# Attention and mixture-of-experts kernel on one core: projections on other slots, three buffers of probabilities, value products in bursts of two key tiles

## The chip, the cores and the metric

The kernel runs on one core of a Trainium2 chip. The metric is the device time of one execution in microseconds (us). A core has TensorE (PE; PEld is its loading of weights), VectorE (DVE), ScalarE (ACT) and GpSimd (POOL); SyncE (SP) only issues transfers here. Each runs its own list of instructions in order, and they wait for each other by semaphores.

## The reference

For 8 sequences of 512 tokens of width 256:

```
x = x + tanh(g_xattn) * attention(q=layernorm(x), k=ctx, v=ctx)     # "cross": 16 heads of 16, softmax over 512 keys
z = layernorm(x)
h = z + (causal attention with rotary embedding of rmsnorm(z)*g1, projections wq, wk, wv) @ wo   # "own"
y = h + moe(rmsnorm(h) * g2)                                         # softmax router, best 2 of 8 experts, hidden 704
x = x + tanh(g_ffn) * y
```

All is float32. The experts compute (silu(t @ wg) * (t @ wu)) @ wd.

## The kernel before

**Attention.** There are 16 units of attention, 8 cross and 8 own, in the order of `UNITS` (cross of sequence b+2, then own of b). A unit has 4 groups of 4 heads. The program goes in steps -1 to 7 of 8 **stages** each, s0 to s7. A stage holds 16 **slots** (4 key tiles `kt` by 4 heads `hd`). Slot numbers in the tables run through a step: slot 16 s + 4 kt + hd. In each stage three groups are in work:

- the maxima of one group (`max_unit`): PE multiplies queries with keys into one of 3 banks `max_ps`, and DVE reduces each to a row maximum (`neg`, L1274). Stages s0 to s3 do this for a cross unit (512 keys), s4 to s7 for an own unit (128 to 512 keys, plus a small product with a mask).
- the main work of a group whose maxima are two stages old (`key_unit`, `exp_unit`, `value_unit`): PE makes the transposed scores in one of 2 banks `key_ps`; the maxima are three extra rows of `q_stack`. ACT takes the exponential into `probs` (L1155), and PE multiplies the values with the probabilities into `pv_ps` (L984), four heads side by side in 32 columns of the array each. In s0 and s1 that is an own unit, in s2 to s5 a cross unit, in s6 and s7 an own unit.
- between both, the maxima are split in three by POOL (`split_neg`, L1604 to L1607), turned by PE (L997, after `kt` 1), copied by ACT to `neg_rows` (L1230, before `kt` 2) and sent to `q_stack` by a DMA. `key_unit` of the next stage waits for it. A finished group is copied to `out_t` (L1225), turned by PE (L1009) and divided by DVE (`post_norm`).

The four value products of a key tile stand after slot `hd` 1 of the next key tile:

```
if hd == VALUES_AT:
    for each in range(HG):
        if kt == 0 and tail: value_unit(step, tail, QT - 1, each)
        if kt and mn:        value_unit(step, mn, kt - 1, each)
```

**Everything else** is put on slots by hand. `X_TURNS`, `HN1_TURNS`, `Q_HALVES`, `K_HALVES`, `V_HALVES`, `WO_HALVES`, `LOGITS`, `RANKS` and the like say at which slot of which step PE begins a transpose or a half of a projection. They all go through one bank, `aux`, one after the other: `aux_turn` makes PE wait until the one before is taken out, which ACT does two slots after a transpose (`evacuate`, L1161), and DVE three slots after a half of q or k (`rotation`: a product with the cosines, L1311, and a shuffle, L1313, which frees the bank). POOL multiplies, adds and splits what DVE left in `turned` and `with_cos` (`rotate`, L1614, L1615), at the stages of `ROTATE_STAGES`. POOL also splits inputs and the experts' weights (`split_piece`), normalises rows (`hn2_rows`, `x1_rows`), adds up (`base_rows`) and scatters rows; `HN2_STAGE`, `BASE_STAGE`, `SCATTER_STAGES` and `PIECES_IN_STEP` give the stages. SP loads the stacks of the next units (`load_stack`, six DMAs each) and waits for `key_ps` products before each.

**Experts.** After the last step the rows are gathered by expert in 71 tiles of 128, each with an up product, a gate and a down product, PE after PE.

Of the kernel before, what the change touches and what calls it, by code (L numbers as in the profile page):

```python
# [20 lines left out]
ALU = mybir.AluOpType  # L21
# [8 lines left out]
E, F = 8, 704  # L30
# [28 lines left out]
VALUES_AT = 1  # L59

# [76 lines left out]
def stage(i, s):  # L137
# [6 lines left out]
X_STATS = {b: at(b - 4, 68) if b > 2 else at(-1, 36) for b in range(2, B)}  # L144
X_TURNS = {1: at(-1, 2, 6), 2: at(-1, 50, 54), 3: at(0, 44, 48), **{b: at(b - 3, 4, 8) for b in range(4, B)}}
C_TURNS = {1: at(-1, 26, 30), 2: at(-1, 66, 70), 3: at(0, 52, 56), **{b: at(b - 3, 26, 30) for b in range(4, B)}}
X1_SUMS = {b: at(b - 2, 118, 128) for b in BATCHES} | {0: at(-1, 112, 114), 1: at(0, 46, 48), LAST: at(LAST - 2, 112, 114)}
X1_ENDS = {b: at(b - 1, 4) for b in BATCHES} | {0: at(-1, 116), 1: at(0, 50), LAST: at(LAST - 2, 116)}
HN1_ROWS = {b: at(b - 1, 20) for b in BATCHES} | {0: at(0, 0), 1: at(0, 60), LAST: at(LAST - 1, 0)}
HN1_TURNS = {b: at(b - 1, 72, 76) for b in REGULAR_OWN} | {0: at(0, 4, 8), LAST - 1: at(LAST - 2, 44, 48), LAST: at(LAST - 1, 4, 8)}  # L150
Q_HALVES = {b: at(b - 1, 80, 85) for b in REGULAR_OWN} | {0: at(0, 12, 17), LAST - 1: at(LAST - 2, 52, 57), LAST: at(LAST - 1, 12, 17)}
K_HALVES = {b: at(b - 1, 105, 117) for b in REGULAR_OWN} | {0: at(0, 22, 27), LAST - 1: at(LAST - 2, 82, 87), LAST: at(LAST - 1, 22, 27)}
V_HALVES = {b: at(b, 33, 38) for b in BATCHES} | {LAST - 1: at(LAST - 2, 118, 123), LAST: at(LAST - 1, 33, 38)}
ATT_TURNS = {b: at(b + 1, 52, 56) for b in BATCHES} | {LAST - 3: at(LAST - 2, 62, 66), LAST - 1: at(LAST - 1, 114, 118), LAST: at(LAST, 48, 52)}
WO_HALVES = {b: at(b + 1, 60, 66) for b in BATCHES} | {LAST - 3: at(LAST - 2, 70, 75), LAST - 1: at(LAST - 1, 122, 128), LAST: at(LAST, 56, 61)}
# [3 lines left out]
LOGITS = {b: at(b + 1, 98) for b in BATCHES} | {LAST - 3: at(LAST - 2, 102), LAST - 1: at(LAST, 27), LAST: at(LAST, 87)}
CHOICES = {b: at(b + 1, 100, 102, 104) for b in BATCHES} | {LAST - 3: at(LAST - 2, 104, 106, 108), LAST - 1: at(LAST, 29, 31, 33),  # L160
                                                          LAST: at(LAST, 89, 91, 93)}
RANKS = {b: at(b + 1, 110) for b in BATCHES} | {LAST - 2: at(LAST - 1, 107), LAST - 1: at(LAST, 36), LAST: at(LAST, 96)}
PLACES = {b: at(b + 1, 113, 115, 122) for b in BATCHES} | {LAST - 2: at(LAST - 1, 109, 110, 112), LAST - 1: at(LAST, 39, 40, 41),
                                                         LAST: at(LAST, 98, 99, 100)}

XQ_STAGE = {b: stage(b - 4, 4) if b > 2 else stage(-1, 2) for b in range(2, B)}
# [7 lines left out]
HN2_STAGE = {b: stage(b + 1, 4) for b in BATCHES} | {LAST - 3: stage(LAST - 2, 5), LAST - 1: stage(LAST, 0), LAST: stage(LAST, 4)}  # L174
BASE_STAGE = {b: stage(b + 1, 5) for b in BATCHES} | {LAST - 1: stage(LAST, 1), LAST: stage(LAST + 1, 0)}
SCATTER_STAGES = {b: (stage(b + 2, 5), stage(b + 2, 6)) for b in BATCHES} | \
    {LAST - 4: (stage(LAST - 2, 2), stage(LAST - 2, 3)), LAST - 3: (stage(LAST - 1, 2), stage(LAST - 1, 4)),
     LAST - 2: (stage(LAST - 1, 7), stage(LAST, 0)), LAST - 1: (stage(LAST, 3),) * 2, LAST: (stage(LAST, 7),) * 2}
PIECES_IN_STEP = {-1: (0, 0, 1, 1, 1, 1, 1, 1), 0: (2, 0, 0, 0, 1, 2, 2, 2), LAST - 2: (0, 0, 2, 2, 0, 0, 2, 1),
                  LAST - 1: (2, 0, 0, 2, 1, 2, 2, 1), LAST: (0,) * 8}  # L180


def pieces_in(st):

    count = lambda n: PIECES_IN_STEP.get(n // 8, (0, 0, 0, 2, 3, 2, 1, 0))[n % 8]
    done = sum(count(n) for n in range(stage(-1, 0), st))
    return range(done, done + count(st))
# [86 lines left out]
def flamingo_block(nc, x, ctx, g_xattn, g_ffn, wq, wk, wv, wo, w_router, wg, wu, wd, g1, g2, out):  # L274
# [25 lines left out]
    with outer:  # L300
# [23 lines left out]
        with ExitStack() as st:  # L324
# [20 lines left out]
            probs = s1("probs", 2, HG, S)  # L345
# [18 lines left out]
            turned = {"q": s1("turned_q", DC, S), "k": s1("turned_k", DC, S)}  # L364
            with_cos = {"q": s1("with_cos_q", DC, S), "k": s1("with_cos_k", DC, S)}
# [377 lines left out]
            def _(sp):  # L743
# [87 lines left out]
                def body(step):  # L831
# [12 lines left out]
                    if i + 3 < B:  # L844
                        load_ctx(i + 3)
# [910 lines left out]
```

## Time and profile before

| | |
|---|---|
| times of three runs | 1591.45, 1581.02, 1590.68 us, median 1590.68 us |
| profiled execution | 1575.98 us, of which the span of instructions is 1573.6 us |
| PE, PEld, DVE, ACT, POOL busy in the span | 1433.8, 881.3, 975.2, 777.3, 879.7 us |
| stretch of attention, 40 to 1023 us | PE busy 918.77, DVE 673.77, ACT 593.38, POOL 714.83 us |
| between attention and experts, 1023 to 1078 us | PE busy 17.88 us, its clock 0.53 of full speed |
| experts, 1078 to 1573.6 us | PE busy 482.50 us |
| mean TensorE clock | 0.976 |

A busy share is the time in which an engine had an instruction in work. A matmul's span in the trace includes its way through the array; how much time it takes from its engine is the distance from its start to the start of the next. The start of each copy to `out_t` (once in a stage, at `kt` 1) is used as a mark, so a stretch between two marks is one stage long; the stretch called s3 runs from `kt` 1 of s2 to the end of `kt` 0 of s3. In step 2 the marks stand at 373.57, 388.15, 400.64, 415.43, 430.65, 447.30, 463.29, 481.07 and 494.83 us.

### The profile page before, as it was taken

The numbers are of one execution on the slowest core, as the hardware profiler recorded it, in microseconds if no ns is written. First come the engines' busy times: TensorE is split into PE (matmuls) and PEld (weight loads), VectorE is DVE, ScalarE is ACT, GpSimd is POOL, SyncE is SP. The second block draws the span as 40 slices with busy tenths as digits, with TensorE's granted clock in tenths as the row PEclk, the third lists the DMA queues.
The fourth block names the chain that finished last, engine by engine and source line by source line (L and its number), as shares of the span: only waits on it lengthen the run. The fifth ranks groups of instructions, "written<-read, shape, count | busy, mean of one in ns | idle before, by whom it ended". The sixth has DMA issues, their size and how long they took to land.

```text
span 1573.6 us, 31721 instructions
## 1 busy us (share of the span) xinstructions
PE 1433.8 (91%) x9439; PEld 881.3 (56%) x9439; DVE 975.2 (62%) x2329; ACT 777.3 (49%) x1782; POOL 879.7 (56%) x1147
## 2 busy tenths in 40 slices
PE   3999999999999999999899998845999999999997
PEld 1232334344444444444444454434999999999996
DVE  5888767757767766766866656324555555555553
ACT  1576665665665664665566555611333333333332
POOL 7485776974977977877879676533222222222222
PEclk9999999999999999999999999957999999999999
DMA  7665356565565574664553646146252454355220
GB/s 198 187 173 174 106 177 180 169 209 143 153 204 166 167 218 148 180 181 163 175 187 103 210 136 192 68 166 207 38 150 53 136 151 143 47 152 149 40 42 11
DMA packets 116517, 230.19 MB, mean 146 GB/s; under 512 B 20101, under 2 KB 82949, under 8 KB 114310
## 3 DMA queue, kind: packets, MB, share of 16 engines
q1 hardware_dynamic: 76114, 147.65, 31.2%
q0 software_dynamic: 26032, 69.82, 15.8%
q10 hardware_dynamic: 14212, 10.71, 2.7%
q8 instruction: 86, 1.41, 0.4%
q14 instruction: 73, 0.60, 0.1%
HBM read 135.10 MB, written 93.14 MB: 145 GB/s over the span
## 4 chain that ended last, share of the span: by engine, by line
PE 68%; POOL 9%; DVE 8%; issue 5%; ACT 4%; DMA 4%; SPq 1%; ACTq 0%; POOLq 0%; DVEq 0%
PE pv_ps L984 9%; PE pv_ps L713 9%; PE max_ps L689 9%; PE key_ps L689 9%; PE max_ps L946 8%; PE key_ps L963 8%; DVE neg L1274 4%; PE aux L1032 3%; PE aux L1023 3%; ACT probs L1155 2%; PE turn_ps L702 2%; PE aux L1016 2%; POOL rows_in L1681 2%; DMA q_stack<-neg_rows 2%; POOL w_parts L1578 1%
## 5 line engine op out<-in xcount | busy, mean ns | idle before, releaser
L1274 DVE TENSOR_REDUCE neg<-max_ps 128x1 f32<-128x512 f32 (+3 forms) x864 | 543.5, 666 | 278.9 <-PE max_ps L949 177.3
L1155 ACT ACTIVATE probs<-key_ps 128x512 f32<-128x512 f32 (+3 forms) x1024 | 497.1, 519 | 366.8 <-PE key_ps L963 176.1
L946 PE MATMUL max_ps<-k_stack,q_stack 96*128 96x512 bf16 (+3 forms) x1024 | 356.1, 352 | 30.8 <-DVE neg L1274 16.2
L963 PE MATMUL key_ps<-q_stack,k_stack 99*128 99x512 bf16 (+3 forms) x1024 | 350.3, 343 | 24.4 <-ACT probs L1155 16.0
L556 POOL DMA_INDIRECT out<-part,whose x71 | 110.1, 1551 | 377.4 <-DVE part L589 304.9
L946 PEld LDWEIGHTS max_ps<-k_stack,q_stack 96*128 96x128 bf16 x1024 | 100.8, 99 | 219.3 <-DVE neg L1274 123.0
L963 PEld LDWEIGHTS key_ps<-q_stack,k_stack 99*128 99x128 bf16 x1024 | 100.2, 98 | 131.0 <-ACT probs L1155 70.0
L713 PE MATMUL pv_ps<-weights,hidden_t 128*128 x1207 | 161.9, 288 | 1.4 <-DVE hidden_t L609 1.4
L689 PE MATMUL max_ps<-weights,rows_t 128*128 x642 | 153.7, 385 | 2.8 <-DVE rows_t L580 2.8
L689 PE MATMUL key_ps<-weights,rows_t 128*128 x636 | 150.3, 381 | 1.0 <-DVE rows_t L580 1.0
L713 PEld LDWEIGHTS pv_ps<-weights,hidden_t 128*128 128x128 f32 x1207 | 149.0, 191 | 1.7 <-issue 1.7
L984 PE MATMUL pv_ps<-probs,v_cross 128*32 128x512 f32 (+3 forms) x1024 | 132.3, 588 | 3.4 <-ACT out_t L1225 2.3
L689 PEld LDWEIGHTS max_ps<-weights,rows_t 128*128 128x128 f32 x642 | 117.8, 191 | 22.9 <-issue 3.2
L689 PEld LDWEIGHTS key_ps<-weights,rows_t 128*128 128x128 f32 x636 | 115.1, 189 | 20.2 <-issue 1.2
L949 PE MATMUL max_ps<-squares_b 128*128 128x128 bf16 x512 | 113.2, 221 | 0.0
L966 PE MATMUL key_ps<-squares_b 128*128 128x128 bf16 x512 | 112.6, 220 | 0.0
L653 ACT ACTIVATE hidden_t<-turn_ps 128x512 fp32r<-128x512 f32 x71 | 42.4, 597 | 135.5 <-PE turn_ps L702 133.3
L984 PE MATMUL pv_ps<-probs,v_own 128*32 128x512 f32 (+3 forms) x1024 | 102.6, 470 | 3.1 <-ACT out_t L1225 2.0
L1604 POOL TENSOR_SCALAR neg_parts<-neg 128x16 bf16<-128x16 f32 x64 | 16.0, 250 | 154.9 <-DVE neg L1274 145.8
L1578 POOL TENSOR_TENSOR w_parts<-w_in,w_parts 128x704 fp32r<-128x704 f32 (+2 forms) x64 | 85.9, 1343 | 5.4
L628 ACT ACTIVATE rows_t<-max_ps,g_sb 128x128 fp32r<-128x128 f32 x142 | 44.4, 364 | 85.7 <-PE max_ps L666 65.6
L609 DVE TENSOR_TENSOR hidden_t<-turn_ps,hidden_t 128x512 fp32r<-128x512 f32 x71 | 49.1, 692 | 45.6 <-ACT hidden_t L653 45.6
(213 smaller groups left out, 2102.1 us busy)
## 6 DMA issues: line engine op xcount, KB each, us to landing
w_split<-w_parts POOLq DMA_DIRECT2D x32, 704.0 KB, 5.6
weights<-w_split SPq DMA_DIRECT2D x8, 2816.0 KB
weights<-w_split SPq DMA_DIRECT2D x8, 1280.0 KB
rows<-rows_in ACTq DMA_DIRECT2D x71, 129.0 KB, 2.1
w_split<-w_parts POOLq DMA_DIRECT2D x16, 512.0 KB, 3.6
kept_sb<-kept SPq DMA_DIRECT2D x16, 512.0 KB, 6.1
parts_cross_k<-parts_k SPq DMA_DIRECT2D x48, 128.0 KB
parts_cross_q<-parts_q SPq DMA_DIRECT2D x48, 128.0 KB
```

The lines of the kernel that those rows point to most:

```text
L556: g_.indirect_dma_start(out=out_rows, out_offset=bass.IndirectOffsetOnAxis(ap=whose[j % OWNERS][:, 0:1], axis=0), in_=part[j % OWNERS][:, ...
L609: v.tensor_tensor(lo[:, 0:4, :].rearrange("p k t -> p (k t)"), hid_ps[0][:, :], hi[:, 0:4, :].rearrange("p k t -> p (k t)"), ALU.subtract) ...
L689: r = mm(ps, rows_t[:, a, c, :], weights[:, bass.ds(off + (w_ * WALL + c * 2 * F + n0), n1 - n0)], start=(c == 0 and (a, w_) == PASSES[0]) ...
L713: r = mm(y_ps[:, 0:D], hidden_t[:, a, k, :], weights[:, bass.ds(off + (w_ * WALL + 2 * WG + k * D), D)], start=(k == 0 and (a, w_) == PASS ...
L946: r = mm(ps[:, 0:keys], q_stack[g][0:KROWS, hd, qt * P:(qt + 1) * P], k_stack[g][0:KROWS, hd, 0:keys], start=True, stop=not own)
L949: r = mm(ps[:, qt * P:keys], ident_b, mask_qk, start=False, stop=True)
L963: r = mm(ps[:, q0:S], k_stack[g][0:KROWS + NEGROWS, hd, kt * P:(kt + 1) * P], q_stack[g][0:KROWS + NEGROWS, hd, q0:S], start=True, stop=no ...
L966: r = mm(ps[:, q0:q0 + P], ident_b, mask_kq, start=False, stop=True)
L984: mm(pv_ps[32 * hd:32 * hd + 32, q0:S], v_of[value_tile(which, b)][:, kt, g * HG + hd, :], probs[:, kt % 2, hd, q0:S], start=(kt == 0), st ...
L1155: act.activation(probs[:, kt % 2, hd, q0:S], key_ps[j % 2][:, q0:S], ACT.Exp).then_inc(m["exp_done"], 1)
L1274: v.tensor_reduce(neg[:, g % 2, hd - place_:hd + 1, qt], scores, op=ALU.max, axis=AX.X, negate=True).then_inc(m["max_red"], many)
L1578: chain.link(g_.tensor_tensor(low, whole, high, ALU.subtract))
```

## The change

- `probs` has three places (`PROBS = 3`) in place of two, used in turn by all key tiles. The value products of two key tiles stand behind each other: those of tiles 0 and 1 after slot `hd` 1 of `kt` 2, those of 2 and 3 after slot `hd` 1 of `kt` 0 of the next stage.
- The slots of the side work are others. In a middle step the attention output's transposes and `wo` go from s3 and s4 to s5 and s6, the halves of q from s5 to s7, the halves of k from s6 and s7 to s0 and s1 of the next step, the second half of v from s2 to s3, `hn2`, router and ranks one step later from s5 to s7 to s4 to s6. POOL's `hn2_rows` and `base_rows` go to s7, and the weight pieces per stage are other numbers of the same total.
- To make room, `turned` and `with_cos` exist once, and not for q and k each; `rotation` waits for POOL to have read the half two before.
- The evacuations of `hn1` and `hn2` (four per sequence) go from ACT to DVE (`take_out`).
- The DMA of `neg_rows` is issued by SP and not by ACT.
- SP's `send_base` of the last steps stands elsewhere.

```diff
+PROBS = 3
-HN1_TURNS = {b: at(b - 1, 72, 76) for b in REGULAR_OWN} | ...
-Q_HALVES = {b: at(b - 1, 80, 85) for b in REGULAR_OWN} | ...
-K_HALVES = {b: at(b - 1, 105, 117) for b in REGULAR_OWN} | ...
+HN1_TURNS = {b: at(b - 1, 92, 95) for b in REGULAR_OWN} | ...
+Q_HALVES = {b: at(b - 1, 112, 120) for b in REGULAR_OWN} | ...
+K_HALVES = {b: at(b, 10, 24) for b in REGULAR_OWN} | ...
...
-            probs = s1("probs", 2, HG, S)
+            probs = s1("probs", PROBS, HG, S)
-            turned = {"q": s1("turned_q", DC, S), "k": s1("turned_k", DC, S)}
-            with_cos = {"q": s1("with_cos_q", DC, S), "k": s1("with_cos_k", DC, S)}
+            turned, with_cos = s1("turned", DC, S), s1("with_cos", DC, S)
...
+                def send_neg(step, s):
+                    unit = step.neg_of(s)
+                    if unit:
+                        n = unit[2] * G + unit[3]
+                        sp.wait_ge(m["neg_ev"], n + 1)
+                        sp.dma_start(q_stack[unit[3]][KROWS:KROWS + NEGROWS, :, :], neg_rows[:, :]).then_inc(m["neg_dma"], 16)
...
-                       probs[:, kt % 2, hd, q0:S], start=(kt == 0), stop=(kt == QT - 1), skip_group_check=True)\
+                       probs[:, (n * QT + kt) % PROBS, hd, q0:S], start=(kt == 0), stop=(kt == QT - 1), skip_group_check=True)\
...
-                                if hd == VALUES_AT:
-                                    for each in range(HG):
-                                        if kt == 0 and tail:
-                                            value_unit(step, tail, QT - 1, each)
-                                        if kt and mn:
-                                            value_unit(step, mn, kt - 1, each)
+                                if hd == VALUES_AT and kt % 2 == 0:
+                                    unit = mn if kt else tail
+                                    for k in (0, 1) if kt else (2, 3):
+                                        for each in range(HG) if unit else ():
+                                            value_unit(step, unit, k, each)
...
-                    step.wait(act, m["pv_mm"], n * 16 + (HG * (kt - 2) + hd + 1))
+                    step.wait(act, m["pv_mm"], n * 16 + (HG * (kt - PROBS) + hd + 1))
...
-                                step.wait(act, m["neg_ev"], n + 1)
-                                act.dma_start(q_stack[ng[3]][KROWS:KROWS + NEGROWS, :, :], neg_rows[:, :]).then_inc(m["neg_dma"], 16)
...
-                    over(dve, m["rope_used"], 4 * (b - 1) + k + 1)
+                    over(dve, m["rope_used"], 4 * b + k - 1)
...
+                def take_out(name, b, c, dst, scale):
+                    aux_full(dve, name, b, c)
+                    v.tensor_scalar(dst[:, c, :], aux[:, :], scale[:, c:c + 1], None, ALU.mult).then_inc(m["aux_free"], 1)
```

On PE, in a cross stage with cross maxima, the program before has a burst of four value products after every four pairs of `max_ps` and `key_ps` products:

```order
L984 MATMUL pv_ps<-probs,v_cross_57 32x512 x4
L946 MATMUL max_ps2<-k_stack2_55,q_stack2_51 128x512
L963 MATMUL key_ps0<-q_stack0_49,k_stack0_53 128x512
L946 MATMUL max_ps0<-k_stack2_55,q_stack2_51 128x512
L963 MATMUL key_ps1<-q_stack0_49,k_stack0_53 128x512
L1009 MATMUL turn_ps<-ident,out_t 128x128 x4
L946 MATMUL max_ps1<-k_stack2_55,q_stack2_51 128x512
L963 MATMUL key_ps0<-q_stack0_49,k_stack0_53 128x512
L946 MATMUL max_ps2<-k_stack2_55,q_stack2_51 128x512
L963 MATMUL key_ps1<-q_stack0_49,k_stack0_53 128x512
L984 MATMUL pv_ps<-probs,v_cross_57 32x512 x4
```

The changed program has eight there (two key tiles), and no burst for the next eight pairs; here half of them are shown, with the second half of v between:

```order
L1018 MATMUL pv_ps<-probs,v_cross_57 32x512 x8
L1066 MATMUL aux<-sb_wv,hn1_t 128x256 x2
L980 MATMUL max_ps1<-k_stack3_56,q_stack3_52 128x512
L997 MATMUL key_ps0<-q_stack1_50,k_stack1_54 128x512
L1066 MATMUL aux<-sb_wv,hn1_t 128x256 x2
L980 MATMUL max_ps2<-k_stack3_56,q_stack3_52 128x512
L997 MATMUL key_ps1<-q_stack1_50,k_stack1_54 128x512
L980 MATMUL max_ps0<-k_stack3_56,q_stack3_52 128x512
L997 MATMUL key_ps0<-q_stack1_50,k_stack1_54 128x512
L980 MATMUL max_ps1<-k_stack3_56,q_stack3_52 128x512
L997 MATMUL key_ps1<-q_stack1_50,k_stack1_54 128x512
L980 MATMUL max_ps2<-k_stack3_56,q_stack3_52 128x512
```

So half of the switches between scores and value products are gone, and the stretch of scores between two bursts is twice as long.

On PE in s1 of a middle step (own keys, cross maxima), the changed program has the second half of k (`sb_wk`), the burst, one pair, and then the transpose of `ctx_in` into the same bank `aux`:

```order
L1057 MATMUL aux<-hn1_t,sb_wk 128x512
L980 MATMUL max_ps0<-k_stack1_54,q_stack1_50 128x512
L997 MATMUL key_ps1<-q_stack3_52,k_stack3_56 128x256
L1000 MATMUL key_ps1<-squares_b 128x128
L1018 MATMUL pv_ps<-probs,v_own 32x512 x4
L1018 MATMUL pv_ps<-probs,v_own 32x384 x4
L980 MATMUL max_ps1<-k_stack1_54,q_stack1_50 128x512
L997 MATMUL key_ps0<-q_stack3_52,k_stack3_56 128x256
L1000 MATMUL key_ps0<-squares_b 128x128
L1050 MATMUL aux<-ident,ctx_in_59 128x128 x4
L980 MATMUL max_ps2<-k_stack1_54,q_stack1_50 128x512
L997 MATMUL key_ps1<-q_stack3_52,k_stack3_56 128x256
```

Before, the halves of k stand in s6 and s7 with no user of `aux` for twelve slots behind the second; here the next user comes at slot 27, the very slot at which DVE takes the half of k out.

On ACT, at `kt` 2 of each stage, the program before has the copy of the turned maxima and the issue of their DMA in a row:

```order
L1155 ACTIVATE probs<-key_ps1 128x512
L1230 ACTIVATE neg_rows<-turn_ps 48x128
L1232 DMA q_stack3_52<-neg_rows 3x16x128
L1155 ACTIVATE probs<-key_ps0 128x512
L1155 ACTIVATE probs<-key_ps1 128x512
```

The changed program has the DMA in SP's list, here between the six DMAs of a stack load and the next ones:

```order
L784 DMA k_stack2_55<-parts_cross_k 48x1x2048
L784 DMA k_stack2_55<-parts_cross_k 32x1x2048
L784 DMA k_stack2_55<-parts_cross_k 16x2048
L830 DMA q_stack0_49<-neg_rows 3x16x128
L789 DMA parts_own_q<-parts_q_61 8x16x512 x6
L784 DMA q_stack3_52<-parts_cross_q 48x1x2048
L784 DMA q_stack3_52<-parts_cross_q 32x1x2048
L784 DMA q_stack3_52<-parts_cross_q 16x2048
```

The issue is off ACT and stands in a queue that waits for other things too.

## Rows read from the trace of the kernel before

**Rows 1.** View by stretches, step 2, s0 to s7: length, each engine's busy us (instructions), clock, DMA.

```profile
373.57:388.15 14.58, 13.21 (x103) 6.20 (x101) 12.64 (x30) 7.25 (x19) 4.24 (x8) 1.00 0.44 121
388.15:400.64 12.49, 11.99 (x93) 5.63 (x93) 11.73 (x25) 8.29 (x22) 11.11 (x22) 1.00 0.60 168
400.64:415.43 14.79, 13.79 (x98) 6.91 (x96) 10.84 (x19) 9.43 (x25) 13.53 (x17) 1.00 0.74 242
415.43:430.65 15.22, 14.58 (x82) 5.81 (x81) 10.81 (x19) 10.31 (x21) 13.79 (x16) 1.00 0.32 87
430.65:447.30 16.65, 16.42 (x98) 7.73 (x96) 9.71 (x18) 10.35 (x21) 10.99 (x13) 1.00 0.77 219
447.30:463.29 15.99, 15.02 (x97) 6.56 (x97) 10.92 (x26) 11.94 (x29) 12.51 (x17) 1.00 0.63 211
463.29:481.07 17.78, 16.98 (x120) 8.56 (x119) 8.48 (x17) 10.39 (x22) 16.14 (x26) 1.00 0.64 207
481.07:494.83 13.76, 12.89 (x122) 6.72 (x120) 10.76 (x41) 7.18 (x20) 8.91 (x15) 1.00 0.40 125
sum 121.26, PE 114.88 PEld 54.12 DVE 85.91 ACT 75.13 POOL 91.21; mean PE 14.36 PEld 6.76 DVE 10.74 ACT 9.39 POOL 11.40
```

**Rows 2.** Timeline of PE in stretch s3 of step 2: start us, us, instruction, count.

```profile
424.60 0.38 PE L963 MATMUL key_ps<-q_stack,k_stack 99*128 99x512 bf16 x1
424.91 1.06 PE L984 MATMUL pv_ps<-probs,v_cross 128*32 128x512 f32 x8
425.91 0.39 PE L946 MATMUL max_ps<-k_stack,q_stack 96*128 96x512 bf16 x1
```

**Rows 3.** Timeline of PE in step 7, bursts of an own group.

```profile
1002.18 1.07 PE L984 MATMUL pv_ps<-probs,v_own 128*32 128x512 f32 x8 [0.18 <-ACT out_t L1225]
...
1009.93 0.43 PE L984 MATMUL pv_ps<-probs,v_own 128*32 128x128 f32 x8
```

**Rows 4.** Timeline of PE's weight loads around one burst.

```profile
510.86 0.16 PEld L984 LDWEIGHTS pv_ps<-probs,v_own 128*32 128x32 f32 x8 [0.21 <-ACT probs L1155]
```

**Rows 5.** Timeline of PE, side work and the next instruction.

```profile
458.30 1.02 PE L1023 MATMUL aux<-hn_t,sb_wq 128*128 128x512 f32 x2
459.16 0.22 PE L946 MATMUL max_ps<-k_stack,q_stack 96*128 96x128 bf16 x1
...
474.00 0.66 PE L1016 MATMUL aux<-ident,hn 128*128 128x128 f32 x4
474.49 0.38 PE L946 MATMUL max_ps<-k_stack,q_stack 96*128 96x512 bf16 x1
```

**Rows 6.** View by groups, shapes apart, whole span: busy us, mean ns, idle before.

```profile
L1274 DVE TENSOR_REDUCE neg<-max_ps 128x1 f32<-128x512 f32 x640 | 411.4, 684 | 121.6 <-PE max_ps L946 98.3 <-PE max_ps L949 21.3
L1155 ACT ACTIVATE probs<-key_ps 128x512 f32<-128x512 f32 x640 | 356.3, 599 | 224.5 <-PE key_ps L963 176.1 <-PE key_ps L966 46.1 <-ACT neg_rows L1230 0.9
...
L1614 POOL TENSOR_TENSOR turned_q<-turned_q,rope_sb 128x512 f32<-128x512 f32 x16 | 20.9, 1307 | 0.2
...
L1313 DVE STREAM_SHUFFLE turned_k<-aux 128x512 f32<-128x512 f32 x16 | 11.8, 738 | 0.0
...
L1311 DVE TENSOR_TENSOR with_cos_k<-aux,rope_sb 128x512 f32<-128x512 f32 x16 | 10.9, 681 | 0.0
```

**Rows 7.** Waits from 374 to 495 us: who for whom, total us, times, longest.

```profile
PEld key_ps L963 <- ACT probs L1155: 6.6, 17, 0.9
```

**Rows 8.** View of line 1232, the issue of the maxima's DMA: ns min/median/max.

```profile
L1232 ACTq DMA_DIRECT2D q_stack<-neg_rows x64: 728/729/900, 45.1 to 1005.1; - x64
```

**Rows 9.** Timeline of PE in stretch s6 of step 3.

```profile
591.08 0.24 PE L997 MATMUL turn_ps<-squares_b,neg_parts 128*48 128x128 bf16 x1 [2.30 <-POOL neg_parts L1607]
```

**Rows 10.** View by stretches: s6 of step 3, and 2 us in it.

```profile
584.64:605.81 21.17, 18.58 (x120) 9.23 (x119) 8.69 (x17) 10.49 (x22) 18.77 (x29) 0.92 0.60 181
594.00:596.00 2.00, 2.00 (x10) 1.33 (x10) 0.56 (x1) 0.24 (x1) 1.99 (x3) 0.50 0.30 61
```

**Rows 11.** Waits of SP's queue from 374 to 495 us.

```profile
SPq L776 <- PE key_ps L963: 34.5, 5, 12.2
```

More of the change, by code:

```diff
@@ L142 @@
 REGULAR_OWN = range(1, LAST - 1)
-X_STATS = {b: at(b - 4, 68) if b > 2 else at(-1, 36) for b in range(2, B)}
+X_STATS = {b: at(b - 4, 84) if b > 3 else at(-1, 68 if b == 3 else 36) for b in range(2, B)}
 X_TURNS = {1: at(-1, 2, 6), 2: at(-1, 50, 54), 3: at(0, 44, 48), **{b: at(b - 3, 4, 8) for b in range(4, B)}}
-C_TURNS = {1: at(-1, 26, 30), 2: at(-1, 66, 70), 3: at(0, 52, 56), **{b: at(b - 3, 26, 30) for b in range(4, B)}}
-X1_SUMS = {b: at(b - 2, 118, 128) for b in BATCHES} | {0: at(-1, 112, 114), 1: at(0, 46, 48), LAST: at(LAST - 2, 112, 114)}
@@ L159 @@
[L159 to L164, printed above, removed]
@@ L166 @@
-XQ_STAGE = {b: stage(b - 4, 4) if b > 2 else stage(-1, 2) for b in range(2, B)}
+HN1_TURNS = {b: at(b - 1, 92, 95) for b in REGULAR_OWN} | {0: at(0, 4, 8), LAST - 1: at(LAST - 2, 46, 50), LAST: at(LAST - 1, 4, 8)}
+Q_HALVES = {b: at(b - 1, 112, 120) for b in REGULAR_OWN} | {0: at(0, 12, 17), LAST - 1: at(LAST - 2, 54, 59), LAST: at(LAST - 1, 12, 17)}
+K_HALVES = {b: at(b, 10, 24) for b in REGULAR_OWN} | {0: at(0, 26, 34), LAST - 1: at(LAST - 2, 78, 83), LAST: at(LAST - 1, 26, 34)}
+V_HALVES = {b: at(b, 34, 50) for b in BATCHES} | {0: at(0, 41, 50), LAST - 2: at(LAST - 2, 33, 41), LAST - 1: at(LAST - 2, 118, 123),
+                                                  LAST: at(LAST - 1, 44, 49)}
@@ L167 @@
+XQ_STAGE = {b: stage(b - 4, 5) if b > 3 else stage(-1, 4 if b == 3 else 2) for b in range(2, B)}
 X_STAGE = {1: stage(-1, 0), 2: stage(-1, 4), **{b: stage(b - 3, 2 + (b == 3)) for b in range(3, B)}}
@@ L836, in body @@
                     if i == LAST:
+                        send_neg(step, 0)
                         send_base(LAST - 1)
@@ L865, in body @@
                     load_stack(step.half(1), 0)
+                    send_neg(step, 3)
                     if i + 4 < B:
@@ L874, in body @@
                     load_stack(step.half(1), 1)
+                    send_neg(step, 4)
                     if i + 3 < B:
@@ L877, in body @@
                     load_stack(step.half(1), 2)
+                    send_neg(step, 5)
                     if i == LAST - 2:
@@ L881, in body @@
                     load_stack(step.half(1), 3)
+                    send_neg(step, 6)
                     if i == LAST - 2:
@@ L886, in body @@
                         load_stack(step.half(2), 0)
+                    send_neg(step, 7)
                     if 0 < i < LAST - 1:
```

108 lines of the change are left out of this document (65 added, 43 removed).

## The prediction

> **What bounds the kernel now.** I read the page first (busy shares, then the clock row), then the view by stretches over one middle step, then timelines and waits within it. Attention runs to 1023 us and the experts from 1078 us; the change touches only the first part. In a middle step of 121.26 us PE is busy for 114.88 us, DVE for 85.91, ACT for 75.13 and POOL for 91.21 [rows 1]. So PE sets the step, but not in all stretches. The lengths go from 12.49 to 17.78 us, and the long ones (s4 16.65, s6 17.78) are those with most side work on PE: 16.42 and 16.98 us busy. In s0 and s1 the maxima are those of a cross unit and DVE has 12.64 and 11.73 us of work in 14.58 and 12.49: there DVE sets the pace and PE waits for banks, much of it in pieces too short to be idle in this view. In s6 POOL has 16.14 of 17.78. A saving on PE therefore counts in six stretches of eight, and hardly in s0 and s1.
>
> **Bursts of two key tiles.** What a switch costs: the last scores product before a burst starts at 424.60 and needs 0.22 us for its 512 columns (the spacing of such products here), so it is through at 424.82, and the next scores product starts at 425.91 [rows 2]: 1.09 us. The own bursts of 512 and of 128 columns last 1.07 and 0.43 us [rows 3], so 384 columns are worth 0.64 and 512 columns 0.85. The rest of 1.09 is 0.24, paid at each switch. Two tiles in a row pay it once. There are 64 groups with 4 bursts now and 2 then, so 128 switches go: 128 x 0.24 = 31 us of PE time. Of that three quarters lie in stretches that PE sets: **-23 us** (bounds -31, and 0 if the second tile can't follow without a gap).
>
> For the second tile to follow at once its weights must be loaded under the first one's products. In the trace all eight loads of a burst lie within 0.16 us at its start, the products take 1.06 [rows 2, 4]; so loads that use the same 128 rows and the same 32 columns do go under running products. The Trainium skill (TensorE: Matmul & The Clock Gate, Part 3, The mechanism) says that loading overlaps with running matmuls only when the row group differs; here all four heads use all rows. By that rule the gap between the two tiles would stay. By it the term would be 0; the trace speaks against the rule.
>
> **Longer stretches of scores.** Between bursts stand eight pairs and not four. An exponential of 512 columns takes 356.3/640 = 0.56 us of ACT's time [rows 6], a pair of PE only 2 x 0.22 = 0.44, and there are just two banks `key_ps`. So far a burst of 1.1 us let ACT catch up after four pairs. Now a burst of 1.9 us leaves ACT idle for 0.8 of it (two banks hold 1.1 us of work), and over eight pairs PE would run 8 x 0.12 = 1.0 us ahead and must wait. In the 8 half stages of a step with cross keys that is at most 8 us a step if nothing else stood between; but the turns of maxima and outputs and 1.3 us of side work on average stand in each half stage, and they give ACT that time. I take 1 us a step, **+8 us** for eight steps (bounds 0 and +40, the latter if side work covers only a third).
>
> **ACT's relief.** Each of the 64 issues of the maxima's DMA holds ACT for 0.73 us [rows 8] while exponentials wait, and four evacuations per sequence leave too. PE's loads waited 6.6 us for exponentials in that step [rows 7]. I take a third of it, 2 us a step: **-16 us** (bounds 0 and -53, all of it). The four evacuations cost DVE 0.68 each (a pass of the same size from a bank, [rows 6]), in s4 to s6, where DVE has 9.71, 10.92 and 8.48 us of work in 16 to 18 [rows 1]: nothing; in a stage that DVE sets they would cost 2.7 a step.
>
> **Levelling of the stretches.** `wo` and its transposes leave s4 (4 x 0.86 + 2 x 0.49 = 4.4 us by [rows 5]) for s5 to s7, the halves of k come to s1 and s2. Work that PE does in another stretch which PE sets too saves nothing. What saves is that the arithmetic of `PLACES` and half of `X1_SUMS` leave stretch s0, which DVE sets: s0 is 2.1 us longer than s1 with the same main work [rows 1], of which 0.7 is more side work on PE. I take the other 1.4 over five steps: **-7 us** (bounds 0 and -12). That s1 gets 1.7 us more of PE work and two passes of DVE (0.68 + 0.74) is on the other side and in the next term.
>
> **The bank `aux`.** Side work now follows itself more closely. At slot 27 PE wants `aux` for `ctx_in`, and at slot 27 DVE takes out the second half of k: DVE must first do the maximum of slot 26 (411.4/640 = 0.64), then 0.68 and 0.74 [rows 6], after a PE that reaches the place some 0.2 us after that maximum's scores. PE stops for about 1.9 us, where before it had twelve slots of distance. Slots 10, 86 to 98 have distances of 0 or 1 slot behind ACT or DVE, where two were the rule; I put 0.3 us on each of five. Together 3.4 us a step, five steps: **+17 us** (bounds 0, if PE would have waited for DVE there anyway, and +30).
>
> **POOL.** In step 3, `split_neg` came late, PE stood still for 2.30 us [rows 9], and the clock fell to half for some us (0.50, 1.2 GHz, from 594 to 596 us); that stretch took 21.17 us against 17.78 for the same one in step 2 [rows 1, 10]. `hn2_rows` and `base_rows` leave the full stages 4 and 5 for 7, where POOL has only 8.91 us of work. I count this case and half of one more: **-6 us** (bounds 0 and -12). SP takes over 64 issues; its queue waits 34.5 us of the step for keys to be read [rows 11], and the maxima have half a stage, 7 us, to land: nothing (bounds 0 and +20, if a store ahead in its queue is late by more than that).
>
> **Sum.** -23 + 8 - 16 - 7 + 17 - 6 = -27 us, against the profiled execution's 1575.98 us: 1549 us. The three runs have a median of 1590.68 us, 14.7 above the profiled one. I read the difference as more cases like step 3's (3.4 us each), of which POOL's relief removes about half: 1590.7 - 27 - 7.5 = **1556 us**.
>
> **Rivals.**
> *More than that* (0.15): the waits on `aux` lie where DVE sets the pace anyway, and ACT's relief gives 4 us a step: 1556 - 17 - 16 = 1523. For it speaks that s1 is DVE's; against it that slot 27 lies at the border of s2, which PE sets.
> *The clock falls at slot 27* (0.12): a wait of 1.9 us is close to the 2.30 after which it fell. Half clock for some 3 us costs 1.7 each time; in five steps, with waits of 1 us more behind it, +13: 1569.
> *The gaps stay* (0.15): the second tile's loads do not go under the first one's products, or the longer stretches cost what the bursts give. 23 us of gain are lost: 1579.
> *Slower: one buffer of rotation* (0.13). DVE's `rotation` of the first half of k at slot 13 must wait until POOL has read the first half of q in stage 0, of the second half at slot 27 until POOL has read that of q in stage 1. POOL needs two products of 1.3 us [rows 6] and two passes no longer than these, 5.2 us at most. It has 13/16 of a stage, 10.6 us, in the first case and 11/16, 9 us, in the second. With `hn2_rows`, `base_rows` and a weight piece now in s7 and two rotations in s1 (11.11 us of 12.49, [rows 1]), a POOL that is 4 us late or more makes DVE wait, and behind it the maxima and PE. If it is 6 us late, each case costs 2 us and half clock 1.7: 7.4 a step, six steps and their echo in the next maxima's split together +50: 1606. It decides from a lateness of 4 us on. Against it: POOL has 91.21 of 121.26 us of work, and the same total after.
> *The forecast* (0.45): 1556.
>
> **Range and chances.** Below 1520 I see only the bounds of ACT's term; above 1592 most of the slower rival. Leaving out both, the range is 1520 to 1592. About 1% (1575 to 1607) is what a measurement of this kernel can tell from no change. Faster by over 1%: the forecast's 0.45 less a tenth of it, 0.15, and nine tenths of the clock's 0.12: 0.66. Slower by over 1%: 0.08 of the slower rival and 0.02 from the gaps: 0.10. Within 1%: 0.24.
>
> **What would show it.** In the changed profile: 128 bursts with 16 products, of 1.9 us for cross groups (the gap's term wrong if 2.1 or more); a middle step of about 117 us with stretches from 13 to 16; PE idle of about 1.9 us before the transpose of `ctx_in` at slot 27; no half clock at `split_neg`; waits of PE for exponentials around 5 us a step. The prediction is wrong if DVE waits for POOL's `rope_used`, if `key_ps` products wait for the maxima's DMA, or if the waits for exponentials grow beyond 10 us a step.

## The result and the profile after

The changed kernel takes 1673.59 us (median of 4 runs, 1669.86 to 1674.14) against 1589.92 us before; the ratio is 1.0541, 95% interval 1.0511 to 1.0570: slower. Forecast were 1556 us, and even the slower rival's 1606 lay far below what came. In the profiles nearly all of it is lost in attention, which ends at 1119 us where it ended at 1023. The profiled execution of the kernel before was a quick one of its kind (1575.98 us against a median of 1589.92), so the profiles differ by 98 us and the medians by 84.

The view by stretches of the changed kernel, step 2, in the columns of [rows 1]:

```profile
390.79:405.33 14.54, 12.75 (x101) 6.64 (x102) 11.73 (x26) 7.16 (x19) 9.86 (x17) 1.00 0.33 104
405.33:422.20 16.87, 14.83 (x97) 6.90 (x95) 11.92 (x23) 8.04 (x21) 15.26 (x25) 0.90 0.60 178
422.20:441.67 19.47, 15.30 (x103) 7.76 (x100) 12.28 (x23) 9.54 (x25) 14.06 (x18) 1.00 0.54 168
441.67:457.21 15.54, 14.42 (x78) 5.47 (x77) 10.71 (x19) 9.80 (x21) 14.12 (x15) 1.00 0.37 105
457.21:470.58 13.37, 12.56 (x83) 5.11 (x83) 9.46 (x16) 9.64 (x21) 5.02 (x9) 1.00 0.47 149
470.58:490.64 20.06, 17.59 (x117) 7.67 (x116) 9.78 (x33) 9.39 (x21) 9.36 (x14) 0.83 0.68 198
490.64:510.05 19.41, 16.45 (x117) 8.66 (x115) 11.13 (x31) 10.39 (x21) 7.57 (x15) 1.00 0.32 98
510.05:524.94 14.89, 14.06 (x114) 7.88 (x113) 14.53 (x29) 8.79 (x27) 12.30 (x17) 1.00 0.65 223
sum 134.15, PE 117.97 PEld 56.09 DVE 91.54 ACT 72.76 POOL 87.54; mean PE 14.75 PEld 7.01 DVE 11.44 ACT 9.10 POOL 10.94
```

The step is 12.9 us longer than in [rows 1], of which PE is busy for only 3.1. The stretches are no more level than before: s4 fell by 3.3 us, but s1, s2, s5, s6 and s7 rose by 4.4, 4.7, 4.1, 1.6 and 1.1. The clock column has left 1.00 in s1 and s5.

The same view over all of attention, from the first copy to `out_t` to the last, first of the kernel before, then of the changed one:

```profile
68.66:1022.86 954.20, 891.92 (x6161) 412.86 (x6159) 649.71 (x1373) 580.69 (x1310) 697.89 (x982) 0.99 0.55 166
```

```profile
71.49:1119.45 1047.96, 917.60 (x6161) 434.34 (x6159) 671.75 (x1402) 565.39 (x1279) 699.65 (x981) 0.95 0.49 151
```

Of 93.8 us, 68 are idle time of PE (62.3 us before, 130.4 after) and 26 are more busy time. The granted clock shows 10.2 us at its lower level (1.2 GHz, called half clock below) in this part before, 102.4 us after. How much half clock one execution has varies: among the 18 of the kernel before that were timed with e1, the time goes from 1582.44 us at a mean clock of 0.975 to 1590.84 us at 0.965, and e1 and e9, two kernels within 0.4% of it, both show 30.7 us in attention. So some 20 of the 92 us may be the luck of the profiled execution. What the idle time waits for, from the view of waits over the same stretch of the changed kernel (total us, times, longest):

```profile
PE max_ps L980 <- DVE neg L1295: 33.8, 43, 2.0
PE key_ps L997 <- ACT probs L1188: 29.9, 79, 1.0
PE aux L1050 <- DVE turned L1334: 14.1, 7, 3.5
PE aux L1050 <- DVE hn_t L1404: 7.3, 5, 1.5
```

So two kinds of wait came: for the banks of scores, and for the bank `aux`. Summed over all lines of that view, PE's waits before products into `max_ps` and `key_ps` went from 36 us in the kernel before to 68, those before the uses of `aux` from 6 to 50, the larger part. One place of each, from PE's and DVE's timelines of the changed kernel in step 2 (start us, us, instruction, count, idle before):

```profile
414.42 0.68 DVE L1332 TENSOR_TENSOR with_cos<-aux,rope_sb 128x512 f32<-128x512 f32 x1
...
415.02 0.72 DVE L1334 STREAM_SHUFFLE turned<-aux 128x512 f32<-128x512 f32 x1
415.64 0.24 DVE L1310 RECIPROCAL recip<-turn_ps 128x16 f32<-128x16 f32 x1
415.91 0.42 DVE L1315 TENSOR_TENSOR att_own<-turn_ps,recip 128x256 f32<-128x256 f32 x1
```

```profile
414.84 0.22 PE L1000 MATMUL key_ps<-squares_b 128*128 128x128 bf16 x1
417.08 0.45 PE L980 MATMUL max_ps<-k_stack,q_stack 96*128 96x512 bf16 x1 [2.02 <-DVE neg L1295]
...
432.58 0.63 PE L1050 MATMUL aux<-ident,ctx_in 128*128 128x128 f32 x4 [1.95 <-DVE turned L1334]
```

At slot 13 `rotation` and `post_norm` follow one another on DVE for 1.8 us. PE fills its three banks for maxima and stands for 2.02 us at slot 16, after which everything runs at half clock for a while (417.32: a product of 512 columns holds PE 0.43 us, not 0.22). At slot 27 it stands for 1.95 us behind the rotation, where the prediction had 1.9. The stretches behind these two waits, in the view by stretches:

```profile
417.25:420.65 3.40, 3.40 (x23) 1.31 (x23) 2.07 (x4) 1.20 (x2) 3.14 (x9) 0.50 0.64 184
432.58:442.58 10.00, 9.21 (x64) 5.38 (x64) 7.36 (x13) 5.34 (x13) 5.34 (x9) 1.00 0.59 172
```

The clock fell behind the first and not behind the second, and it is so in each of steps 1 to 4.

### The profile page after: what moved, and what is told of

The parts are those of the page before. It is cut to its first block, busy times and chain, and to the rows that moved or that the text cites. A ratio compares the mean times of both kernels' runs of the same rounds, so it can differ in the third digit from the quotient of the medians.

```text
span 1671.2 us, 31721 instructions
## 1 busy us (share of the span) xinstructions
PE 1458.0 (87%) x9439; PEld 901.7 (54%) x9439; DVE 998.6 (60%) x2361; ACT 761.3 (46%) x1750; POOL 881.6 (53%) x1147
## 3 DMA queue, kind: packets, MB, share of 16 engines
q1 hardware_dynamic: 79378, 148.44, 29.3%
## 4 chain that ended last, share of the span: by engine, by line
PE 68%; DVE 9%; issue 7%; POOL 7%; ACT 4%; DMA 3%; SPq 1%; ACTq 0%; POOLq 0%; DVEq 0%
PE pv_ps L1018 11%; PE pv_ps L721 9%; PE max_ps L697 8%; PE key_ps L697 8%; PE max_ps L980 8%; PE key_ps L997 7%; DVE neg L1295 4%; PE aux L1057 3%; PE aux L1066 3%; PE aux L1050 2%; ACT probs L1188 2%; POOL rows_in L1715 2%; PE turn_ps L710 2%; PE key_ps L1000 1%; PE aux L1121 1%
## 5 line engine op out<-in xcount | busy, mean ns | idle before, releaser
L980 PE MATMUL max_ps<-k_stack,q_stack 96*128 96x512 bf16 (+3 forms) x1024 | 364.4, 359 | 50.0 <-DVE neg L1295 35.3
L997 PE MATMUL key_ps<-q_stack,k_stack 99*128 99x512 bf16 (+3 forms) x1024 | 361.6, 355 | 37.7 <-ACT probs L1188 29.9
L1018 PE MATMUL pv_ps<-probs,v_cross 128*32 128x512 f32 (+3 forms) x1024 | 128.2, 622 | 0.0
L1000 PE MATMUL key_ps<-squares_b 128*128 128x128 bf16 x512 | 116.0, 227 | 0.0
L1018 PE MATMUL pv_ps<-probs,v_own 128*32 128x512 f32 (+3 forms) x1024 | 96.0, 497 | 0.0
```

Source lines behind the costliest of these rows:

```text
L980: r = mm(ps[:, 0:keys], q_stack[g][0:KROWS, hd, qt * P:(qt + 1) * P], k_stack[g][0:KROWS, hd, 0:keys], start=True, stop=not own)
L997: r = mm(ps[:, q0:S], k_stack[g][0:KROWS + NEGROWS, hd, kt * P:(kt + 1) * P], q_stack[g][0:KROWS + NEGROWS, hd, q0:S], start=True, stop=no ...
L1000: r = mm(ps[:, q0:q0 + P], ident_b, mask_kq, start=False, stop=True)
L1018: mm(pv_ps[32 * hd:32 * hd + 32, q0:S], v_of[value_tile(which, b)][:, kt, g * HG + hd, :], probs[:, (n * QT + kt) % PROBS, hd, q0:S], star ...
```

## The experiments

Differences are given as differences of ratios to the kernel before, times 1585 us (its medians in these experiments lie between 1581 and 1586 us). Half clock and waits come from the one profiled execution of each kernel.

**Taking the change apart: e1 to e4.** e2 puts only the bursts into the kernel before. They need more places of probabilities, and there is room for one more head's, so both e1 and e2 have nine places by head; e1 has these alone and is the ground for e2:

```
-probs[:, kt % 2, hd, q0:S]
+probs[:, (n * 16 + HG * kt + hd) % 9, q0:S]
 # e2 also
-if hd == VALUES_AT: ... value_unit(step, mn, kt - 1, each)
+if hd == VALUES_AT and kt % 2 == 0: ... for k in (0, 1): value_unit(step, unit, k, each)
```

> The kernel before with nine places for probabilities by head instead of eight (two per key tile), and nothing else. Both theories expect next to no change, 1580 to 1592 us: the exponentials of a key tile wait for products only in a few places. It is the ground on which the next run stands.

> The kernel before, its slot tables and all side work as they were, with only the products of two key tiles in one burst (nine places by head). Theory 1, the new tables of slots cost the 97 us and the bursts gain what was predicted: 1590 - 23 = about 1567 us (1560 to 1575), half clock in attention as before, some 10 us. Theory 2, the bursts of two tiles cost: the scores queue behind 1.9 us of products, the clock falls in or behind them, and the time is 1610 to 1650 us with over 50 us of half clock.

e1: 1.0021 (1.0005 to 1.0038). e2: 1.0116 (1.0089 to 1.0143), so the bursts alone cost 15 us. Theory 1 falls for this part: they lose even with the old tables. Half clock in attention is 52 us, against 31 in e1.

e3 takes only the two moves between engines (`send_neg` on SP, `take_out` on DVE).

> The kernel before with only two moves between engines: SyncE sends neg_rows instead of ScalarE, and VectorE takes hn1_t and hn2_t out of the bank instead of ScalarE; bursts, tables and buffers as before. The prediction's terms give -16 us for ScalarE's relief, so about 1575 us. Rival: VectorE's reductions are later by two of the removals a step each, or the sent rows arrive behind SyncE's queue, and it is 1595 to 1610 us.

0.9960 (0.9943 to 0.9976): 6 us, not 16.

e4 is the changed kernel with the single bursts put back.

> The changed kernel with its tables, moves and three places, but the products of each key tile in a burst of their own, as before. Theory 1 (tables cost, bursts gain): 1674 + 20 = about 1694 us. Theory 2 (the bursts of two tiles cost): 1600 to 1630 us, and the half clock falls from 102 us to under 40.

1.0218 (1.0187 to 1.0249), 1621.5 us. Both theories hold in part: against e3 the tables, the single buffers and the third place of probabilities cost 41 us, and on top of them two-tile bursts cost 51 more, three times their price in e2. Half clock is 58 us here, 21 us in e3.

**Is it the length of the burst? e5, e6.**

```
+if hd in (1, 3):                       # e5, in the changed kernel
+    for each in range(HG) if unit and kt % 2 == 0 else ():
+        value_unit(step, unit, (0 if kt else 2) + hd // 2, each)
```

> The changed kernel whole, but the 16 products of a burst in two bursts of 8 with two slots of scores between them (first key tile at head 1, second at head 3); everything else, the period of two key tiles and the three places too, as changed. If the length of a burst is what costs (VectorE and ScalarE run out of scores while it lasts, since three and two banks hold less than it, and TensorE then waits for them), the time comes down to the single bursts' 1621 us (1615 to 1635), and TensorE's waits for maxima and exponentials from 63.7 to about 30 us. Rival, the later place of the products is what costs: it stays at 1665 to 1675 us.

1.0552 (1.0510 to 1.0594): no difference from 1.0541. The expectation of my theory of length did not come; that no burst follows for the next six slots is what both kernels have in common. It does not show that length costs nothing, for the split brings the switches back: PE is busy for 936.8 us in attention against 917.6, and idle for 116 us against 130. So the split took some 14 us of waiting away and paid as much in busy time.

> The kernel before with the two moves of e3, and bursts of half the length: products of two heads after head 1, of the other two after head 3. By the theory of length the waits for maxima and exponentials (15.5 and 14.6 us in e3) shrink, and the switches that come back cost 256 times 0.24 us at most half of which shows: 1575 to 1600 us. Rival, the switches cost all of it as the prediction priced them: 1580 + 46 to 61 = 1626 to 1641 us.

1.0811 (1.0779 to 1.0843), 1715 us, worse than even the rival's 1641. A burst of e6, from PE's timeline in an own group:

```profile
274.62 1.05 PE L1008 MATMUL pv_ps<-probs,v_own 128*32 128x512 f32 x4
277.57 0.84 PE L1008 MATMUL pv_ps<-probs,v_own 128*32 128x384 f32 x4
```

Four products (two heads) last 1.05 us, as long as eight (four heads) do in [rows 3]. The four heads write different 32 columns of the array and go side by side; two heads leave half of that unused. By the view by groups, shapes apart, all value products with `probs` are busy for 459 us here and for 235 in e3. Most of what halving costs lies there; the switches are inside the same spans and were not measured apart. And PE is hardly ever without work:

```profile
72.94:1162.56 1089.62, 1081.02 (x6162) 440.69 (x6160) 671.84 (x1402) 579.34 (x1279) 699.82 (x980) 1.00 0.48 145
```

Busy for 1081 of 1090 us, it shows 3.4 us at half clock.

**The bank's turn: e7, e8.** Some thirty numbers of the tables, of this kind:

```
-K_HALVES = {b: at(b, 10, 24)    C_TURNS = ... at(b - 3, 27, 30)
+K_HALVES = {b: at(b, 12, 24)    C_TURNS = ... at(b - 3, 29, 32)
-ATT_TURNS ... at(b + 1, 86, 89)   HN1_TURNS ... at(b - 1, 92, 95)   WO_HALVES ... at(b + 1, 98, 105)
+ATT_TURNS ... at(b + 1, 86, 90)   HN1_TURNS ... at(b - 1, 94, 98)   WO_HALVES ... at(b + 1, 102, 108)
```

> The kernel of e4 (tables of the change, single bursts) with the uses of the bank aux moved apart, where one began in the slot in which the one before it was taken out or one later (slots 27, 30, 34, 86 to 98 of the regular steps, some ten places in steps 5 and 6), and the rotation off slot 13. If the bank's turn is what the tables cost, TensorE's waits at aux fall from 37 to about 15 us and the half clock with them: 1621 - 22 - 12 = about 1587 us (1580 to 1600). Rival, the tables cost by the amount of work in a stretch: 1612 to 1625 us.

> The same tables with the bursts of two key tiles, that is the changed kernel with only slots of side work changed. If the two causes add, 1674 - 34 = about 1640 us; if the spaced tables also take away what makes the long bursts dearer here (52 us) than in the kernel before (15 us), about 1610 us.

e7: 1.0042 (1.0024 to 1.0060), 28 us less than e4, within the range of the bank's theory, which had 34. PE's waits at `aux` fell from 38 to 25 us, those for maxima from 18 to 14, half clock from 58 to 44. The edit does two things, it spaces the uses of `aux` and takes the rotation off slot 13, and they were not tried apart. e8: 1.0258 (1.0225 to 1.0291), 45 us less than the changed kernel; the bursts' price is 34 us in these tables. So the causes do not simply add: with the closer tables the bursts cost 51. Why is not shown; that a DVE kept late by one passes it on to the other would explain it.

**The moves apart: e9, e10.**

> The kernel before with only SyncE sending neg_rows. e3, both moves together, gave 0.996 of the kernel before; the prediction's share for ScalarE's queue (64 sends of 0.73 us) is half of its -16 us. Expected: 1578 to 1584 us if this is the half that gains, 1586 to 1590 if nobody waited for ScalarE there.

> The kernel before with only VectorE taking hn1_t and hn2_t out of the bank. If the gain of e3 is the sends, this one is 1585 to 1595 us, since two of VectorE's slots a step get 0.42 us more in front of its maxima and ScalarE gets them back; if it is the removals, 1578 to 1583.

0.9964 (0.9945 to 0.9982) and 1.0005 (0.9984 to 1.0026): all of the gain is the sends.

**The depth of the rings: e11.** The kernel of e3 with `max_ps` used modulo 2.

> The kernel of e3 (single bursts) with two banks for the scores that maxima are taken from instead of three. The theory of evenness says that the depth of the rings decides what a stretch of scores without products costs: with two banks even four slots are too many, TensorE's waits for maxima rise from 15 us to 60 or more and the time by 4 to 8%, 1640 to 1700 us. Rival, only VectorE's rate matters (it is busy 667 of 956 us): 1580 to 1600 us.

1.0186 (1.0157 to 1.0215). In the view of waits over its attention:

```profile
PE max_ps L971 <- DVE neg L1287: 44.4, 91, 4.4
```

Against 15.5 us in e3. The depth does matter, but waits and time (36 us more) rose less than I had expected.

**K's place alone: e12, e14.**

```
-K_HALVES = {b: at(b - 1, 105, 117) for b in REGULAR_OWN}
+K_HALVES = {b: at(b, 12, 23) for b in REGULAR_OWN}
-C_TURNS ... at(b - 3, 26, 30)   V_HALVES = {b: at(b, 33, 38) ...
+C_TURNS ... at(b - 3, 28, 32)   V_HALVES = {b: at(b, 36, 41) ...
```

> The kernel of e3 with one piece of the change's levelling: the regular K projections at slots 12 and 23 of the next step instead of 105 and 117, with C's turns (28, 32) and V's products (36, 41) moved clear of them, single bursts. The prediction's levelling term says a gain: stage s6 from 17.8 to about 15 us, s1 from 12.5 to 14.5, so 1 to 2 us a step, 1568 to 1576 us. If stages are bound by TensorE alone, nothing moves: 1578 to 1582 us. If the bank's turn or SyncE's loads are in its way, over 1585.

> The kernel of e12 (0.990 of the kernel before) without VectorE's taking out of hn1_t and hn2_t, which in e10 made no difference: 1565 to 1572 us, no different from e12. If VectorE's lighter load matters more where K has moved, up to 4 us less.

e12: 0.9899 (0.9870 to 0.9927), 1566.93 us, the fastest kernel of the study, ahead of the kernel before and the changed one. K's move with its bank kept free gives 10 us over e3. In step 2 it is not s6 that fell, as expected, but s7 and s0, by 3.0 and 2.7 us, while s1 and s3 rose by 2.3 and 1.6. e14: 0.9931 (0.9912 to 0.9949), 5 us behind; the intervals overlap, so whether `take_out` on DVE helps here, as it did not in e10, stays open.

**The last steps: e13.**

> The kernel of e7 with one batch's late chain (norm turns, logits, ranks of the fifth batch) done in step 5 as the kernel before does, so that step 6 has the kernel before's slots again. In e7 steps 0 to 4 took 6 us less than in e3, and steps 5 and 6 took 23 us more (133.2 and 134.7 against 123.2 and 121.4). If the chain that the change puts off by a step costs where it has to be made up, step 6 comes down by 10 to 13 us and step 5 rises by 3 to 6: 1594 - 8 = about 1586 us. Rival, the extra time of the two steps comes from other things there (K at stage 0, pieces on GpSimd): 1590 to 1597 us.

1.0092 (1.0067 to 1.0116), 8 us slower than e7: step 5 rose by 3 us, and step 6 did not fall (137.2 us, 134.7 in e7). Theory fallen. What else of the tables costs the 13 us that separate e7 from e3 stays open.

**What the bursts had covered: e15 to e18.** e15 is e12 with e2's bursts and its nine places.

> The kernel of e12 with the bursts of two key tiles and nine places by head. The theory of evenness gives what e2 cost over e1, 15 us: about 1582 us (1578 to 1590). The prediction's own terms (-23 for switches, +8 for longer stretches) would give 1552 us.

1.0054 (1.0031 to 1.0078): 25 us, more than expected, and far from the prediction's terms. Attention in e12 and in e15 by the view of stretches:

```profile
67.71:1018.10 950.39, 896.39 (x6161) 416.51 (x6159) 670.91 (x1403) 565.86 (x1279) 699.27 (x982) 0.98 0.55 167
```

```profile
68.38:1037.56 969.18, 882.14 (x6161) 424.82 (x6159) 664.96 (x1402) 571.72 (x1279) 697.80 (x981) 0.99 0.54 164
```

PE's products got 14 us shorter, its idle time 33 us longer (54.0 to 87.0). I sorted all of PE's waits for maxima and exponentials by how many pairs stood between them and the burst before. In e12 all of 23.5 us lie within the first four pairs, since a burst follows every four. In e15 37.4 of 52.2 lie later: 17.1 for maxima just before the seventh pair, 14.3 for exponentials at the fifth. In the changed kernel it is 62 of 67.5. Three banks before the seventh pair DVE does `post_norm` (slot 13), two banks before the other ACT copies `out_t` (slot 4). With single bursts a burst stood at slots 13 and 5, right beside both; two-tile bursts stand at slots 1 and 9. So I moved the two passes to the bursts that are left:

```
-if kt == 1 and tail: ... act.activation(out_t[:, :], pv_ps[:, :], ACT.Copy)
+if (kt, hd) == (0, 2) and tail: ... the same
-if (kt, hd) == (3, 1) and tail: post_norm(step, tail)
+if (kt, hd) == (0, 2) and before: post_norm(step, before)     # of the stage before
```

Besides, entries of `X1_SUMS` and `X1_ENDS` are later by two to five slots: in e16 and e18 those of the first two and the last sequence, in e17 those of all.

> The kernel of e15 (1.0054 of the kernel before) with two passes moved beside the bursts that are left: ScalarE copies out_t at head 2 of key tile 0, right after the burst, instead of before key tile 1, and VectorE's post_norm stands at slot 2 of the next stage instead of slot 13. In e15 the waits for maxima stand mostly before the seventh pair after a burst (17.1 of 25.7 us) and those for exponentials before the fifth (14.3 of 26.5), three and two banks behind these two passes, which single bursts at slots 5 and 13 cover. If that cover is what two-tile bursts take away: waits for maxima and exponentials from 48 to about 25 us, 1594 - 23 = about 1571 us. Rival, the uneven flow itself costs, wherever the passes stand: the waits move to other pairs and it is 1588 to 1598 us.

> The changed kernel whole with the same two passes moved. Its waits for maxima and exponentials are 63.7 us, of which 29.7 before the seventh pair and 24.9 before the fifth and sixth. By the theory of the cover they fall by some 35 us, and with less idle time the half clock costs some 10 us less: 1674 - 45 = about 1630 us. Rival, the uneven flow: 1660 to 1680 us.

> Control: the kernel of e12 (single bursts, 0.990 of the kernel before) with the same two passes moved. Single bursts cover both passes in either place (out_t's copy then stands between the bursts at slots 1 and 5, post_norm at slot 18 just after the burst of slot 17): 1563 to 1575 us, no gain. A gain as in e16 would mean that the moved passes help by themselves.

e16: 0.9974 (0.9953 to 0.9995). e17: 1.0349 (1.0289 to 1.0408), 30 us less than the changed kernel. e18: 0.9954 (0.9931 to 0.9978), 9 us more than e12. The waits in e15, then in e16:

```profile
PE max_ps L971 <- DVE neg L1286: 25.7, 58, 1.4
PE key_ps L988 <- ACT probs L1179: 22.6, 53, 1.3
```

```profile
PE max_ps L971 <- DVE neg L1286: 14.8, 34, 0.8
PE key_ps L988 <- ACT probs L1179: 14.5, 39, 2.6
PE turn_ps L1022 <- POOL neg_parts L1633: 13.9, 5, 4.9
```

Expected were about 25 us for the two together; 29.3 came. The time fell by 13 us and not by 23: waits for POOL's `neg_parts` rose from 8.1 to 13.9, and half clock from 27 to 34. With both passes moved, bursts of two tiles cost 3 us over single ones (0.9974 against 0.9954, intervals overlap, and the nine places alone cost as much in e1), where they cost 25 with the passes left in place. Of these 22 us, 13 are what the long bursts gained by the move and 9 what the single bursts lost by it. So the loss of the bursts hangs on where the two passes stand, which is shown for these tables. That it is the lost cover is borne out for the 13 us by where the waits went (before the seventh pair from 17.1 to 2.4 us, at the fifth from 14.3 to 3.6). The other 9 are not explained: the expectation had no change for single bursts. In the changed kernel the move gives back 30 of 51 us; there it has no control with single bursts, and the rest was not tried apart.

## Why the prediction was wrong

The forecast was 34 us below the median before, and the result is 84 to 86 above it. Of the 120 us between them, 66 are the bursts (forecast -23 and +8, measured +51 from e4 to the changed kernel), 47 the rest of the change (forecast -12 in all, measured +35 in e4), and 7.5 the gain that the prediction added for POOL's late cases in the unprofiled runs.

**The step that failed first: "longer stretches of scores", +8 us.** It looked at ACT alone and let the turns and side work between pairs give it time. DVE's three banks for maxima were left out, and that `post_norm` and the copy to `out_t` stand at fixed slots beside bursts that the change removes. Measured: PE's waits for the banks of scores rose by 29 us from e12 to e15 and by 34 from e4 to the changed kernel (33 to 68), and its waits at `aux` by 12 in both cases (9 to 21, 38 to 50), which no term had. In the changed kernel half clock came on top (58 to 102 us). The term's upper bound of +40 was in the text; I took its lower end.

**Bursts of two tiles, -23 us.** The size of a switch was right. In the changed kernel:

```profile
494.94 0.38 PE L997 MATMUL key_ps<-q_stack,k_stack 99*128 99x512 bf16 x1
495.25 1.92 PE L1018 MATMUL pv_ps<-probs,v_cross 128*32 128x512 f32 x16
497.11 0.34 PE L980 MATMUL max_ps<-k_stack,q_stack 96*128 96x384 bf16 x1
```

From 495.16, where the scores are through, to 497.11 it is 1.95 us, against twice 1.09 before [rows 2]: 0.23 saved a pair, 0.24 predicted, and 1.92 us for the burst, 1.9 predicted. The loads of the second tile go under running products:

```profile
495.70 0.13 PEld L1018 LDWEIGHTS pv_ps<-probs,v_cross 128*32 128x32 f32 x4 [0.30 <-issue]
```

Of the rival "the gaps stay" the first half is refuted; its other half, that the longer stretches cost what the bursts give, came true and more. With the first half goes, for this case, the rule of the Trainium skill (TensorE: Matmul & The Clock Gate, Part 3, The mechanism) that weight loads overlap with products only in another row group. The saving was real (PE is busy for 14 us less in e15 than in e12) and bought nothing by itself, as the waiting grew by more.

**The bank `aux`, +17 us.** The place and the wait at slot 27 were right (1.95 for 1.9); of the waits at slots 86 to 98, put at 0.3 each, those seen in step 2 are 0.8, 0.4 and 1.5. Measured are 30 us more waiting at `aux` (9 in e3, 38 in e4), as much as the upper bound of +30. Of these, 18 lie in the five regular steps 0 to 4, 3.5 a step where the term had 3.4; the other 12 lie in steps 5 and 6, which it did not count. Missing was what can follow such a wait: 37 us more at half clock, worth up to 19, an estimate that takes all work there to go half as fast. Spacing the uses and moving K's rotation away from `post_norm` at slot 13 (e7) took back 28 us.

**The clock.** It was a rival with 13 us ("the clock falls at slot 27"). In steps 1 to 4 of the changed kernel PE stands for 1.95 us at slot 27, and the clock falls behind it in none; it falls behind the 2.02 us at slot 16 in all four. With single bursts (e4) the same 1.95 us were followed by half clock in two of the four steps. So the place was wrong, and the length of a wait alone does not decide. In all it fell in 23 places, 92 us more at half clock than in the profile before, which cost at most half of that, 46 us.

**ACT's relief, -16 us.** 6 us, all from the sends (e3, e9, e10). "A third of the waits" was a guess.

**Levelling, -7 us.** The term counted the arithmetic of `PLACES` and `X1_SUMS` and took K's move as a gain of nothing. K's move alone gave 10 us (e12), most of it in s7 and s0; that s0 could be relieved was right, the work that did it was another. What the term counted was not tried apart, and the rest of the new tables loses more than K's move gives.

**POOL, -6 us.** No gain seen: waits for `neg_parts` are 6.7 us in the changed kernel, 6.6 in e3, 7.3 before. The term's own working, one case and a half of 3.4 us, gives 5 and not 6. The 7.5 us added for further such cases in the unprofiled runs had no row: executions of the kernel before differ in their mean clock (0.975 to 0.965 beside e1), and what makes it differ is not known.

**One buffer of rotation** (the slower rival) did not happen on its scale: e7 has the single buffers, and DVE waits for POOL there three times, for 5.4 us in all; in the changed kernel twice, the sign that the prediction named, but small:

```profile
DVE with_cos L1332 <- POOL rest L1585: 4.3, 2, 3.2
```

The direction failed because each rival on the slow side was one cause by itself, while here waits of 1 to 2 us at several kinds of place added up, and some of them took the clock with them.

## What to carry over

Before moving or merging a burst, list what other engines do while it runs. A burst that looks like pure cost can also be the time in which passes at fixed slots are caught up; try moving them with it. Give each use of a shared bank two slots of distance to the engine that frees it, since a wait there can be paid again by the clock. A saving on the busiest engine counts only after the depth of the rings behind it has been checked against the longest stretch without a pause.

## What the runs showed of the hardware

Products with weights of 128 rows and 32 columns, on four different groups of columns, run side by side: 4 products of 512 columns for two heads take 1.05 us, 8 for four heads 1.07, 16 for two tiles of four heads 1.92. The Trainium skill (TensorEngine Tiling (Array Packing), Tiling Modes) lists four independent tiles of 128 rows and 32 columns; these rows agree. The granted clock tends to fall less the more gapless PE runs, in one execution each: 3.4 us at half clock in attention with 9 us idle (e6), 58 with 88 (e4), 102 with 130 (changed). Between 54 and 99 us of idle time there is no order: 10 us with 62 (before), 34 with 54 (e12), 55 with 61 (e18), 27 with 87 (e15). And the clock fell at times with PE busy, as at 475.3 in the changed kernel, with PE busy for 9.85 of the 10.3 us before it; the burst of 16 that starts there took 3.51 us and not 1.92.
